# A four-layer transformer kernel on one core: linear layer in two 16-tile stages, its weights split inside the ternary layer, its rows turned by DMA transposes

## The reference

```python
x = _layernorm(x + ffn(x))                       # bitlinear 512->2048, gelu, bitlinear 2048->512
q = k = x @ Wqk + bqk;  v = silu(x @ Wv + bv);  u = silu(x @ Wu + bu)
q, kh, vh = elu(heads(q)), elu(heads(k)), heads(v)          # 16 heads of 32
kv = einsum('bhnd,bhne->bhde', kh, vh)                      # over all 1024 rows of a batch
out = u * _layernorm(einsum('bhnd,bhde->bhne', q, kv), ln_g, ln_b)
x = _layernorm(x + out @ Wo + bo)
scores = softmax(x @ gate_w.T); topk_w, topk_idx = top_k(scores, 2)
# then the experts: swiglu(x @ w_gate_up[e]) @ w_down[e], summed with topk_w, and the shared expert
```

## Time and profile before

| | before |
|---|---|
| device time, median of 3 (range) | 1971.93 us (1968.43 to 1973.26) |
| profiled execution: own time, span | 1969.48 us, 1967.7 us |
| PE, DVE, ACT, POOL busy | 83%, 62%, 47%, 21% |
| granted TensorE clock, mean | 0.928 |
| from the first DMA of `linw` to the end of the chain in `route` | 1027.49 to 1420.08 us, 392.6 us |

### The profile page before, as it was taken

How to read it: one execution, slowest core, us unless ns; L and a number is a source line. 1 busy time by engine, 2 the same in 40 slices (tenths; PEclk the granted TensorE clock), 3 DMA queues, 4 the chain that set the end, 5 groups by cost and what they waited for, 6 DMA issues and landing times. The chain is left out here.

```text
span 1967.7 us, 34154 instructions
## 1 busy us (share of the span) xinstructions
PE 1626.1 (83%) x12714; PEld 828.2 (42%) x12714; DVE 1210.9 (62%) x2031; ACT 926.9 (47%) x1592; POOL 412.5 (21%) x503
## 2 busy tenths in 40 slices
PE   0488999778899976999966977975399799999897
PEld 0363333235333322444422543443355455666564
DVE  2557898365789847788746776775652243333277
ACT  4354677715467771766625633532322143333232
POOL 0170000037000003123211222123353111111055
PEclk9798999989899998999987988987599899999999
DMA  8000000000000000456537914933500675646344
GB/s 317 1 1 1 2 2 2 1 1 1 2 2 2 2 2 10 82 86 107 88 86 281 341 73 170 338 120 115 199 2 1 239 251 174 199 145 201 116 124 134
DMA packets 153730, 197.79 MB, mean 101 GB/s; under 512 B 93802, under 2 KB 97096, under 8 KB 150880
## 3 DMA queue, kind: packets, MB, share of 16 engines
q1 hardware_dynamic: 142048, 168.08, 27.1%
q0 software_dynamic: 7344, 20.73, 3.8%
q10 hardware_dynamic: 4176, 6.82, 1.0%
HBM read 184.94 MB, written 56.40 MB: 123 GB/s over the span
## 5 line engine op out<-in xcount | busy, mean ns | idle before, releaser
L626 ACT ACTIVATE attn_prob<-attn_ps_t 128x512 f32<-128x512 f32 x576 | 312.6, 596 | 128.0 <-PE attn_ps_t L593 126.3
L645 DVE TENSOR_REDUCE attn_mx<-attn_ps_s 128x2 f32<-128x1024 f32 (+3 forms) x304 | 342.8, 1163 | 41.6 <-PE attn_ps_s L574 37.9
L1947 PE MATMUL sparse_ps_g<-wgate,sparse_xT 128*128 128x352 f16 x1128 | 185.6, 315 | 3.6 <-DVE sparse_xT L2025 3.6
L606 PE MATMUL attn_ps_o<-attn_prob,V 128*32 128x256 f32 x2304 | 174.8, 389 | 3.6 <-ACT attn_prob L626 2.7
L1947 PEld LDWEIGHTS sparse_ps_g<-wgate,sparse_xT 128*128 128x128 f16 x1128 | 105.3, 98 | 74.8 <-DVE sparse_xT L2025 24.8
L1133 PE MATMUL lin_ps_z<-w,lin_xT 128*128 128x512 f16 x576 | 135.7, 386 | 0.0
L593 PE MATMUL attn_ps_t<-QT,KT 64*128 64x256 f16 x1152 | 112.2, 273 | 18.7 <-ACT attn_prob L626 11.4
L873 PE MATMUL ffn_ps_fc<-wfcT,ffn_xT 128*128 128x512 f16 x512 | 114.8, 383 | 15.3 <-DMA ffn_xT<-ffn_x 15.3
L883 PE MATMUL ffn_ps_y<-wprojT,ffn_hT 128*128 128x512 f16 x512 | 117.6, 389 | 7.1 <-DMA ffn_hT<-ffn_h 7.1
L780 POOL TENSOR_TENSOR wo_o<-O,wo_o 128x512 f16<-128x512 f32 (+1 forms) x16 | 18.4, 1155 | 496.1 <-ACT wo_o L752 496.0
L574 PE MATMUL attn_ps_s<-KT,QT 64*128 64x512 f16 (+3 forms) x768 | 115.6, 337 | 2.1 <-DVE attn_mx L645 2.1
(11 more groups left out here) (312 smaller groups left out, 3007.5 us busy)
## 6 DMA issues: line engine op xcount, KB each, us to landing
wgate<-gate_d SPq DMA_DIRECT2D x47, 1408.0 KB
wdown<-down_d SPq DMA_DIRECT2D x47, 768.0 KB
lin_sp_raw<-in_L_ffn_w_gate_up_dram SPq DMA_DIRECT2D x56, 352.0 KB, 5.1
gate_d<-lin_sp_parts SPq DMA_DIRECT2D x56, 352.0 KB, 4.6
y_d<-sparse_y SPq DMA_DIRECT2D x47, 256.0 KB
down_d<-lin_sp_parts SPq DMA_DIRECT2D x42, 256.0 KB, 5.1
lin_sp_raw<-in_L_ffn_w_down_dram SPq DMA_DIRECT2D x28, 256.0 KB, 4.4
prep_w_fc<-in_L_ffn_w_fc_dram SPq DMA_DIRECT2D x4, 1024.0 KB
```

Source lines behind the costliest of these rows:

```text
L606: last = pe.matmul(ps_o[32 * jj:32 * jj + 32, 256 * half:256 * half + 256], V[:, kt, 4 * jg + jj, :], prob[(2 * q + jj // 2) % 4][:, half, ...
L626: act.activation(prob[g % 4][:, par, :, :], ps_t[:, (2 * g + par) % 3, :, :], ACT.Exp, scale=HD ** -0.5).then_inc(exp_done, 1)
L645: dve.tensor_reduce(mx[x % 2][:, c, :, at:at + per], ps_s[:, 2 * (r % 2):2 * (r % 2) + 2, 0:per * n].rearrange("p e (h k) -> p e h k", k=n ...
L1947: last = pe.matmul(ps_g[u][n][rows, :], xT[u][:, a, k, rows], w, start=(k == 0 and i == 0), stop=(k == KC - 1 and i == 2), skip_group_chec ...
```

## The change

1. `linear_weights` goes. Its loads and splits of Wqk, Wv, Wu and Wo are cut into 16 pieces of 128 x 512, one a tile of `ternary_ffn`: SP loads (`next_layer`), ACT makes the high part (`next_high`), DVE the low part (`next_low`). `m.w1` now lies in an arena that the attention's QT and the ternary weights used before it, and half of the shared expert's weights use after.
2. The two `linear_features` become one stage of 16 tiles, with 14 experts beside it. The biases are loaded and split at its start, ahead of the expert loads on SP and ahead of the first `xevac` on DVE. The bias matmul now comes last in its group. The turned x has two PSUM buffers instead of one.
3. The two `linear_output` and `route` become one stage of 16 tiles, `linear_output_and_route`. In it both turns, of the gated rows (`wt`, lag 1) and of the new x (`xt`, lag 5), are DMA transposes from SP, and the PSUM copies of them go. The last 2 experts and the shared half run beside it, 21 pieces in a ring of 4; the shared half is split in 7 pieces straight into its place.

```diff
@@ ternary_ffn
+                def next_layer(t):
+                    i, k = divmod(t, KC)
+                    after(sp, w1l_done, t - 3)
+                    w = d["L1_attn_" + ("Wqk", "Wv", "Wu", "Wo")[i]]
+                    sp.dma_start(raw[t % 4][:, :], w[k * P:(k + 1) * P, :]).then_inc(raw_in[t % 4], 16)
-                unrolled(NT, [(3, xt), (5, ht(0)), (5, ht(1))])
+                unrolled(NT, [(0, next_layer), (3, xt), (5, ht(0)), (5, ht(1))])
...
-                unrolled(NT, [(4, gelu(0, 1, 2, 3)), (5, hhi), (4, square), (2, xhi), (4, h_norm)])
+                unrolled(NT, [(4, gelu(0, 1, 2, 3)), (5, hhi), (4, square), (2, xhi), (4, h_norm), (1, next_high)])
...
-                unrolled(NT, [(5, h_clip), (8, norm), (4, h_mean), (7, residual), (5, hlo), (4, h_var), (0, x_stats), (2, xlo), (1, x_norm)])
+                unrolled(NT, [(5, h_clip), (8, norm), (4, h_mean), (7, residual), (5, hlo), (4, h_var), (0, x_stats), (2, xlo), (1, x_norm), (1, next_low)])
@@
-LIN_EXPERTS = 7
+LIN_EXPERTS = 14
@@ linear_features, SP
+                sp.wait_ge(b_zero, 1)
+                for i, n in enumerate(("bqk", "bv", "bu", "bo")):
+                    for row in (0, LO_ROW):
+                        sp.dma_start(brow[row:row + 1, i, :], d[f"L1_attn_{n}"][None, :]).then_inc(b_in, 16)
                 split.transfers(sp)
@@ linear_features, ACT and DVE
-                unrolled(TB, [(0, of(xhi)), (2, of(nonlinear)), (3, of(kt_hi)), (1, split.spread(split.high, act, TB))])
+                unrolled(NT, [(0, xhi), (0, biases), (2, nonlinear), (3, kt_hi), (3, kv_hi),
+                              (1, split.spread(split.high, act, NT))])
...
-                unrolled(TB, [(1, of(xevac)), (2, of(features)), (3, of(kt_lo)), (1, split.spread(split.low, dve, TB))])
+                unrolled(NT, [(0, biases), (1, xevac), (2, features), (3, kt_lo), (3, kv_lo),
+                              (1, split.spread(split.low, dve, NT))])
@@ linear_output_and_route (new)
+        split = ExpertSplit(f, m, d, 4, LIN_EXPERTS, NE - LIN_EXPERTS, 1)
...
+                def wt(t):
+                    u = t % 2
+                    sp.wait_ge(wl_done, t + 1)
+                    after(sp, y_done, t - 1)
+                    sp.dma_start_transpose(out=wT[u][:, :, :, :].rearrange("p a k c -> p (a k) c"),
+                                           in_=w2[u][:, :, :].rearrange("p a n -> p (a n)")).then_inc(wt_in[u], 16)
+                def xt(t):
+                    u = t % 2
+                    sp.wait_ge(xl_done, t + 1)
+                    sp.dma_start_transpose(out=m.xT3[:, :, :, t * P:(t + 1) * P].rearrange("p a k c -> p (a k) c"),
+                                           in_=x2[u][:, :, :].rearrange("p a n -> p (a n)")).then_inc(xt_in[u], 16)
+                unrolled(NT, [(1, wt), (5, xt), (5, rows), (0, split.spread(split.load, sp, NT)),
+                              (3, split.spread(split.store, sp, NT))])
...
+                unrolled(NT, [(3, wo), (0, q), (7, logit)])
+                unrolled(NT, [(1, whi), (5, xhi), (2, split.spread(split.high, act, NT))])
+                unrolled(NT, [(1, gating), (4, norm), (0, stats), (3, residual), (7, levac),
+                              (2, split.spread(split.low, dve, NT))])
+                unrolled(NT, [(1, wlo), (0, lambda t: ln_q.root(pool, t, t % 2)),
+                              (3, lambda t: ln_r.root(pool, t, t % 2)), (5, xlo)])
@@ build
-            ternary_ffn(nc, m)
+            ternary_ffn(nc, m, d)
-        linear_attention(nc, m, d)
         experts(nc, m, d, out)
```

More of the change, by code:

```diff
@@ L996, with __init__ @@
 PIECES = KC + len(FCH)
-LIN_EXPERTS = 7
+LIN_EXPERTS = 14
 class ExpertSplit:
[L1006 to L1013, removed]
+    def __init__(self, f, m, d, ring, first, count, shared):
+        self.m, self.d, self.ring, self.first = m, d, ring, first * PIECES
+        self.kept, self.count = count * PIECES, (count + shared) * PIECES
+        self.raw = [f.sb(f"sp_raw{u}", [P, 2 * FE], F32) for u in range(ring)]
+        self.parts = [f.sb(f"sp_parts{u}", [P, 2 * 2 * FE], F16) for u in range(ring)]
+        self.raw_in = [f.sem(f"sp_raw_in{u}") for u in range(ring)]
+        self.stored = [f.sem(f"sp_stored{u}") for u in range(ring)]
         self.hi_done, self.lo_done = f.sems("sp_hi_done sp_lo_done")
@@ L1066, in low, with spread @@
         dve.wait_ge(self.hi_done, i + 1)
-        dve.scalar_tensor_tensor(self.part(i, 1), self.raw[i % self.RING][0:rows, 0:width], WS, self.part(i, 0),
+        dve.scalar_tensor_tensor(self.part(i, 1), self.raw[i % self.ring][0:rows, 0:width], WS, self.part(i, 0),
                                  ALU.mult, ALU.subtract).then_inc(self.lo_done, 1)
-    def spread(self, fn, eng, tiles, slot=0, slots=1):
+    def spread(self, fn, eng, tiles):
         def at(t):
-            turn = t * slots + slot
-            for i in range(turn * self.count // (tiles * slots), (turn + 1) * self.count // (tiles * slots)):
+            for i in range(t * self.count // tiles, (t + 1) * self.count // tiles):
                 if t < tiles:
@@ L1182, in kv @@
                         s = slice(g * P, (g + 1) * P)
[L1183 to L1185 removed]
+                        last = pe.matmul(ps_kv[t // TB][:, g, :], relu[u][:, s], tanh[u][:, 0, s],
+                                         start=(t % TB == 0 and g == 0), stop=(t % TB == TB - 1 and g == KC - 1))
                     last.then_inc(kv_done, 1)
@@ L1273, in _, with linear_output_and_route @@
-                run_tiles(pool, TB, [(0, xlo), (2, minus_one)])
-def linear_output(nc, m, b):
-    with Phase(nc, f"lino{b}") as f:
+                    pool.tensor_tensor(relu[u][:, :], e[u][:, :], m.ones[:, 0:1].to_broadcast([P, D]),
+                                       ALU.subtract).then_inc(k_done, 1)
+                unrolled(NT, [(0, xlo), (2, minus_one)])
+def linear_output_and_route(nc, m, d):
+    with Phase(nc, "out") as f:
         w = [f.sb(f"w{u}", [P, D], F32) for u in range(2)]
-        n1 = [f.sb(f"n1{u}", [P, D], F32) for u in range(2)]
-        n2 = [f.sb(f"n2{u}", [P, D], F32) for u in range(2)]
```

476 lines of the change are left out of this document (222 added, 254 removed).

## The result

The changed kernel takes 1917.41 us (median of 4 runs, 1910.08 to 1920.24), the kernel before 1970.18 in the same runs: a ratio of 0.9728, 95% interval 0.9694 to 0.9763. It is faster by 53 us; 1917.0 was forecast.

A forecast was written before the change was run, and what follows sets the result against it. Stages with different bounds (TensorE, DMA, DVE, chains of waits), each with head, tail and barrier: 1.5 + 193.6 + 142.6 = 337.7 against 392.6, -54.9 us from 1969.48 gives 1914.6; the median 2.45 higher, 1917 us, range 1904 to 1944.

The forecast's parts named there:

- The weights inside ffn: In `ffn`: next layer's weight splits are covered mid-stage but not at the head; +1.5 us, from 0.7 to 4.
- The head of the features: Bias loads, their split and the copy of xT put `z(0)` at S + 12.2 us, S being the stage's start.
- The +3: Features' second half: DMA sets the pace, 0.3 to 0.4 us a tile for 8 or 9 tiles, 0 to 6.
- Tiles of 11.1 or more in the second half, with TensorE waiting for the relu: Expected sign in the features: tiles of 10.8 us at first, then 11.1 or more.
- the bound that I had feared: Features: DMA sets the pace once the relu's slack of 0.5 us is used up at tile 5 or so.
- The output stage: Merged output and routing, DVE's tile about 6.8 us: 4.3 + 86.2 + 9.4 + 19 + 3 + 2 + 7.1 + 7.6, plus 4: 142.6 us.
- collisions: Output stage: an allowance of 0.25 us a tile, +4 us.
- The 8.0 us of room: Output stage: 8.0 us free for issue and landing of w's transpose before DVE waits; alone it takes 3.9, at worst 5.1.
- the rival's second part: Late-turn rival (0.22), output stage: TensorE falls to 1.2 GHz between its groups and `wo` takes 5.6 us.
- "DVE waits for `q`": Output stage: named as one of the signs that the prediction is wrong.
- That rival's 1945 us: Late-turn rival (0.22): turned rows landing in 10 us or more and `wo` at 1.2 GHz, both together; 1933 with one.
- The rule weighed: Output stage's turns: skill's rule implies 10.5 us for 8 blocks, over 8.0 free; measured 3.9 us kept the sum.

The follow-up runs named there:

- bias_late: Changed kernel with the bias wait moved to the bias matmul and xT(0)'s copy ahead of the bias split on VectorE; 1913.6 us.
- head2: Changed kernel with the bias wait and VectorE order moved, and on ScalarE the bias's high part behind x(1)'s; 1910.8 us.
- less_dve: Changed kernel without the layer norm's offset and w's scale, 0.69 us less VectorE a tile in the output stage; 1917.4 us.
- split16: Changed kernel with all 16 experts split in the features stage, only the shared expert's 7 pieces in the output stage; 1922.7 us.
- pool_light: Changed kernel with the low part of the output stage's x rows computed by POOL for one column only; 1911.8 us.

## Why the prediction was right, and where by luck

From the start of the features to the end of the chain it took 335.3 us for 336.2, with errors in the parts that are told below. That the median agrees to 0.4 us is luck in part. The sum, 1914.6, was made for the profiled execution, which took 1910.1; the median lies 7.3 us above that execution, where the prediction had added 2.45.

- **The weights inside ffn:** +0.5 us for +1.5 forecast (248.96 to 249.43 from its first statistics to its last norm). That is less than its range of 0.7 to 4. All of it came at the head, behind `xlo(0)`: counted from the stage's start, `fc` of the first tile is 0.6 us later, from the fourth tile on 1.0, and no more after it; the last norm is 0.5 later.
- **The head of the features:** S + 11.4 for 12.2. The size was right and the path was not: I had it end with the bias split on VectorE and the copy of xT; it went over ScalarE, x(1)'s high part, POOL and x(1)'s turn. The bias split was on it only by what it held POOL, 1.6 us. bias_late shows that taking my path away gives nothing, head2 that taking both away gives 6 us.
- **The tiles of the features:** 174.36 us from `z(0)` to the last k^T v but one, for 84.85 + 86.6 + 3 = 174.45. The +3 was made of something else. "Tiles of 11.1 or more in the second half, with TensorE waiting for the relu" is wrong: they take 10.91 throughout (1062.76 to 1073.67, and so on; before 10.82), which is 1.3 us over 15 tiles, and one tile takes 12.27. There ScalarE waited for a piece of an expert, and x's high part stood behind it:

```profile
1121.53 0.63 ACT L1094 ACTIVATE lin_sp_parts<-lin_sp_raw 128x512 f16<-128x512 f32 x1 [2.59 <-DMA lin_sp_raw<-in_L_ffn_w_down_dram]
...
1124.54 0.61 ACT L1196 ACTIVATE lin_x<-X 128x512 f16<-128x512 f32 x1
...
1126.44 0.62 PE L146 MATMUL lin_ps_x<-ident,lin_x 128*128 128x128 f16 x8 [1.19 <-POOL lin_x L1288]
```

So late transfers do reach TensorE, through ScalarE's queue rather than VectorE's, and at this number of experts once. How often they do differs between executions: in less_dve, whose features are the same code, one step took 14.8 us and the stage 2.5 more. split16 shows the bound that I had feared, 14 pieces further. What makes the other 0.09 us a tile was not tried; the bias matmul now closes a group instead of opening it.
- **The output stage:** 142.7 for 142.6, with errors that cancel. Larger: the gap to the first `q` 6.3 (4.3), the last norm to the chain 9.4 (7.1; SP's queue and the store in it were missing). POOL beside the gating cost 7 x 0.63 + 4 x 0.11 = 4.9 and the waits for `q` 4.7, together 9.6 for the 4 of "collisions"; 1.0 of these waits is that for the first `q`. Smaller: 21 low parts 16.7 (19), logit copies 16 x 0.16 = 2.6 (3), and what is left for head and tail, 128.8 - 86.2 - 16.7 - 2.6 - 4.9 - 4.7 - 9.4 = 4.3, for 9.4 + 2: four low parts and eight logit copies, some 4.4 us, lie behind the last tile's statistics, where VectorE has gaps, and I had counted both.
- **The 8.0 us of room:** right as a size, with one term missing. The turns took 3.1 to 7.6 us, all under 8.0, and still VectorE waited for `q` behind three of them, of 7.6, 6.3 and 7.1 us (0.67, 0.34 and 0.19 us at tiles 9, 12 and 15). Their `wo` took 4.18, 5.13 and 4.57 us for the 2.76 of the prediction. Turn and `wo` together are 11.4 to 11.8 us there, over the 10.8 that it had room for, and at most 10.0 at every other tile. So the rival's second part, TensorE at its 1.2 GHz level, came true in six `wo` of sixteen (4.2 to 5.2 us; the stage's mean granted clock is 0.80), and the reason given against it, that TensorE would be busy all the time at that clock, did not hold. "DVE waits for `q`" was named as a sign of being wrong, and it did, though for 1.2 us in all once the pipeline was full. Made later, the turn cost 8 us (11 expected). That rival's 1945 us does not follow from its terms: (2.0 + 10.4 + 5.6 + 1.0 - 0.5) / 2 = 9.25 us a tile is 16 x 2.25 = 36 us more, 1953.
- **The rule weighed:** the Trainium skill, "VectorE: DVE Perf Modes", "The three transpose paths", gives 1309 ns for one block, by which 8 blocks would be an estimated 10.5 us if one followed the other; they landed in 4.4 (median), 6.8 at most, with loads and stores in the same queue. The trace disagrees with this estimate; no run here turns one block alone. The Trainium skill's advice on the same page, "Rules for kernel authors", to take TensorE where a PSUM result is OK, holds or fails here with the copy: by ScalarE, with time to spare, 125.9 us; by VectorE, the pace, 133.7.
- **The seams** brought the gain: before, 1027.49 to 1420.08 were 392.6 us; now 1026.11 to 1361.39 are 335.3, for 336.2 forecast. Loading the weights and both stages of features took 216.9 us (1027.49 to 1145.78 and 1201.49 to 1300.08) and take 192.6; both output stages and `route` took 175.7 and take 142.7. The 2.3 us by which `ffn` starts earlier and the 0.7 behind the routing were in no term.

## What to carry to other kernels

A wait of the engine that isn't the pace is no cost in itself: of 34 us in which TensorE waited for the transposes, under 5 reached VectorE (3.75 at a `q` and 1.2 at the last residual), and the way to know is to follow the wait to who waits behind it. When two loops are within a tenth of each other, taking work from the first gives back only part (0.69 us a tile brought 3.8 us of 11), so work out the second loop's room before removing anything. At a stage's head, follow every queue that leads to the first matmul; here an operation for the *next* tile stood ahead of it.

## What the runs showed of the hardware

- A VectorE operation on two operands in SBUF was held by a POOL operation beside it: 0.75 us alone (`ln_gb` and w), 1.38 when it started with 0.8 us of POOL's subtraction left, 0.86 with 0.3 us left; a norm, from SBUF to SBUF with one large operand, 0.54 and 1.37. The residual, which reads PSUM and X, kept its 0.68 beside POOL's other subtraction. It works both ways: POOL's subtraction of 1.15 us took 2.73 when it started beside VectorE's bias split. In pool_light, without POOL's subtraction, all sixteen operations took 0.75 and the norms 0.54. The Trainium skill, "SBUF — State Buffer", "SBUF: two separate sides", says that the two engines share a pair of ports and that the one that comes later waits, where the VectorE operation has two inputs in SBUF or is in a mode that uses both ports; the trace agrees for the gating, and for the residual, whose one SBUF input leaves it free.
- SP was held by the issue of a 256 KB transpose of w for 1.23 us at the least, as at the start of the output stage, and for 2.56 at the most, in the middle with the DMA engines at 0.86 (of x for up to 2.80); what stands behind in program order starts only then.
- TensorE's granted clock fell in some groups after a wait for wT, not in all: after 3.55 us at tile 3 `wo` still took 2.76. Two windows of the changed kernel, over a `wo` that followed a wait of 4.2 us and one that followed 0.8 us (columns as in the first fence):

```profile
1266.90:1270.90 4.00, 4.00 (x11) 1.46 (x12) 3.81 (x13) 1.56 (x3) 2.51 (x3) 0.57 1.00 255
1287.60:1290.40 2.80, 2.78 (x13) 1.18 (x13) 2.69 (x8) 1.83 (x3) 1.39 (x2) 1.00 0.76 187
```

The first ran near the level of 1.2 GHz and took 4.45 us, the second at 2.4 GHz and took 2.76. Where the clock falls, a late turn is paid for twice.
